# A selective scan beside a mixture of experts: rows added into a DRAM sum, blocks from tile 45 at five tiles each

## The reference

```python
xn = layernorm(x)                                   # x: 2 x 2048 x 256, 4096 tokens in all
delta = softplus(xn @ W_delta.T + delta_bias)       # 256 channels
B_sel, C_sel = xn @ W_B.T, xn @ W_C.T               # 256 channels x 16 states
# for each token in turn, each channel and state:
h = exp(delta*A) * h + (exp(delta*A) - 1)/A * B_t * x_t
y_t = sum over the 16 states of h * C_t
# mixture of 8 experts on the same xn, top 2 per token:
scores = xn @ Wr + br;  w = softmax over the top two
out = sum over the two of w_e * (gelu(xn @ W1[e] + b1[e]) @ W2[e] + b2[e])    # 256 -> 1024 -> 256
result = x + y + out
```

## Time and profile before

| | us |
|---|---|
| median of the runs shown (3 runs) | 1361.06 (1361.04 to 1361.42) |
| the profiled execution's own time | 1359.79 |
| its span, first to last instruction | 1358.1 |
| PE busy | 1196.7 (88%) |
| DVE busy | 917.0 (68%) |
| ACT busy | 819.2 (60%) |
| POOL busy | 758.9 (56%) |
| mean granted TensorE clock | 0.971 |

### The profile page before, as it was taken

One profiled execution on the slowest core, in us unless ns is written; L12 is line 12 of the kernel. 1 busy time (PEld: TensorE's weight loads), 2 busy tenths in 40 slices (PEclk: granted clock), 3 DMA queues, 4 the chain that ended last, 5 costly groups with the idle time before them and its releaser, 6 DMA issues.

```text
span 1358.1 us, 21913 instructions
## 1 busy us (share of the span) xinstructions
PE 1196.7 (88%) x7674; PEld 730.3 (54%) x7674; DVE 917.0 (68%) x1263; ACT 819.2 (60%) x1379; POOL 758.9 (56%) x557
## 2 busy tenths in 40 slices
PE   1567877878899999999999999999999999997664
PEld 0443323333366666666666666666666666663221
DVE  6867878878966566556665565665656655677677
ACT  3655676576487665767666775767666585752110
POOL 2629999999544544354453535435353444446883
PEclk9979999999999999999999999999999999999777
DMA  6693555565324344443334444344444444323651
GB/s 203 200 309 129 180 188 175 190 198 177 118 85 141 125 136 131 152 143 122 125 121 141 140 142 138 125 140 137 125 127 137 152 138 133 106 86 113 190 156 61
DMA packets 95369, 198.03 MB, mean 146 GB/s; under 512 B 13472, under 2 KB 69152, under 8 KB 85280
## 3 DMA queue, kind: packets, MB, share of 16 engines
q1 hardware_dynamic: 89120, 179.91, 41.6%
q0 software_dynamic: 6144, 16.79, 3.7%
HBM read 143.19 MB, written 53.48 MB: 145 GB/s over the span
## 4 chain that ended last, share of the span: by engine, by line
PE 63%; POOL 6%; DVE 3%; issue 2%; DMA 0%; ACT 0%; POOLq 0%; DVEq 0%; SPq 0%
PE bank L1097 31%; PE bank L1161 15%; PE bank L1146 15%; POOL k_xT L946 5%; POOL ax L915 2%; DVE hb L1004 1%; PE bank L1126 1%; PE bank L1172 1%; DVE bank L991 0%; PE bank L1182 0%; DMA ys<-stage 0%; DVE base L1059 0%; DVE base L1043 0%; DVE bank L1016 0%; ACT state L814 0%
## 5 line engine op out<-in xcount | busy, mean ns | idle before, releaser
L915 POOL TENSOR_TENSOR ax<-ax,x 128x512 f32<-128x512 f32 x256 | 325.7, 1274 | 455.6 <-ACT ax L809 452.4
L1097 PE MATMUL bank<-k_xT,k_WB 128*128 128x512 f16 x1536 | 390.1, 392 | 99.1 <-DVE hb L1004 91.4
L991 DVE TENSOR_TENSOR bank<-ax,bank 128x512 f32<-128x512 f32 x256 | 177.8, 695 | 374.6 <-PE bank L1097 238.8
L1097 PE MATMUL bank<-k_xT,k_WC 128*128 128x512 f16 x1536 | 383.5, 387 | 0.7 <-DVE ysum L1026 0.7
L1097 PEld LDWEIGHTS bank<-k_xT,k_WB 128*128 128x128 f16 x1536 | 144.4, 100 | 278.1 <-DVE hb L1004 134.0
L1097 PEld LDWEIGHTS bank<-k_xT,k_WC 128*128 128x128 f16 x1536 | 153.3, 100 | 192.1 <-issue 17.4
L802 ACT ACTIVATE aexp<-k_dcur,k_A 128x512 f32<-128x512 f32 x256 | 180.7, 711 | 109.8 <-DVE hb L1004 106.5
L1004 DVE TENSOR_TENSOR_SCAN hb<-aexp,state,bank 128x512 f32<-128x512 f32 x192 | 244.6, 1274 | 0.0
L1016 DVE SCALAR_TENSOR_TENSOR bank<-hb,k_rA,bank 128x512 f32<-128x512 f32 x240 | 180.0, 750 | 2.4 <-DVE hb L1004 0.9
L1026 DVE TENSOR_TENSOR ysum<-ysum,bank 128x512 f32<-128x512 f32 x240 | 158.8, 662 | 0.0
L809 ACT ACTIVATE ax<-aexp 128x512 f32<-128x512 f32 x256 | 156.9, 614 | 0.0
(11 more groups left out here) (129 smaller groups left out, 1118.0 us busy)
## 6 DMA issues: line engine op xcount, KB each, us to landing
k_x<-wsplit SPq DMA_DIRECT2D x78, 1024.0 KB, 5.1
stage<-in_W SPq DMA_DIRECT2D x32, 512.0 KB, 4.7
wsplit<-stage SPq DMA_DIRECT2D x32, 512.0 KB, 3.2
xs<-k_zero SPq DMA_DIRECT2D x1, 9984.0 KB, 32.0
stage<-xs SPq DMA_DIRECT2D x39, 256.0 KB, 5.0
ys<-stage SPq DMA_DIRECT2D x39, 256.0 KB, 5.7
stage<-in_b SPq DMA_DIRECT2D x39, 128.0 KB, 5.4
k_x<-in_x SPq DMA_DIRECT2D x4, 1024.0 KB, 9.9
```

Source lines behind the costliest of these rows:

```text
L915: nc.gpsimd.tensor_tensor(ax[:, g % MR], ax[:, g % MR], x32[:, hf], ALU.mult).then_inc(ax_done, 1)
L991: v.tensor_tensor(bank, ax[:, g % MR], bank, ALU.mult).then_inc(ux_done, 1)
L1097: ins = mm(bank[:], W[:, a, kc, n, hf * P:(hf + 1) * P], xT[:, c, b, kc, :], start=(k == 1), stop=(k == 3 * KC))
```

## The change

Seven things change together.

- The 64 scatters carry 1040-byte rows: 256 floats' worth of xn and four more, the token's number + 1, its first slot, and the two weights in the form w0 and w1 - w0. `xs` is 260 floats wide, and so is the zeroing DMA. The prologue writes the four columns.
- Five small DVE operations per block (`slot_op`, 128x2 elements) work out from these the weight of each slot and the row of the sum to which it goes (rows beyond the tokens for empty slots). POOL multiplies the block's output by the weights (`add_block`) and adds it into the DRAM tensor `acc` with two accumulating indirect DMAs. `acc` is filled with x by one DRAM-to-DRAM DMA at tile E0 - 3. Each add waits until the ones before it have landed.
- The scan's rows of chunks 0 to 6 are added into `acc` by an accumulating DMA from POOL (`add_rows`), 512 KB each. `ys`, `mid`, the gathers, `add_expert` and the loads and stores around them are gone. At the end `acc` is copied to the output by two DRAM-to-DRAM DMAs, and the last chunk's rows are loaded, completed on DVE and stored.
- E0 = 45, STEP = 5; `down` is cut in three steps of 18, 15 and 15 matmuls; the turn of the next block is at the block's fourth tile. z and the row turns are made by half, and put in a block's first two tiles (`quiet`).
- The 32 pieces of W go at one per 1.25 tiles, with 4 load buffers and 2 store buffers; the odd pieces' low part is made by DVE, the even ones' by POOL. The 64 scatters go at 1.6 per tile (tiles 0 to 39).
- Softplus is made for each half by itself (L829 to L841 before), so there are 14 of them for chunks 1 to 7. The prologue makes `dcur` for both halves.
- `ax` has 4 buffers in place of 5, `ysum` one in place of two, and ACT no longer waits for the zeroing.

```diff
-E0 = 74
-STEP = 4
+E0 = 45
+STEP = 5
+DOWN_AT = (0, 6, 11, 16)
+W_BUF, HL_BUF = 4, 2
...
+def quiet(g):
+    while E0 - 2 <= g < E_END and (g - E0) % STEP > 1:
+        g += 1
+    return g
+Z_AT = {quiet(c * TILES + 13 + 15 * hf): (c + 1, hf) for c in range(NCH - 1) for hf in range(KC)}
+ROW_AT = {quiet(c * TILES + 21 + 16 * hf): (c, hf) for c in range(NCH) for hf in range(KC) if (c, hf) < (NCH - 1, 1)}
...
+def piece_step(k):
+    return k * 5 // 4
+def scatter_step(j):
+    return j * 5 // 8
+def row_add_step(c):
+    return (c + 1) * TILES + (20 if c == 0 else 14)
+def block_add_step(b):
+    return E0 + STEP * b + 13
...
# SP
-        load_piece(0)
-        load_piece(1)
+        for k in range(W_BUF):
+            load_piece(k)
         for g in range(TILE_N):
+            for k in range(SPLITS):
+                if piece_step(k) + 4 == g:
+                    store_piece(k)
+                    if k + W_BUF < SPLITS:
+                        load_piece(k + W_BUF)
+            if g == E0 - 3:
+                sp.dma_start(acc_rows, io["x"].rearrange("b l d -> (b l) d")).then_inc(acc_set, 16)
+                for r in range(HL_BUF):
+                    sp.wait_ge(piece_out[r], SPLITS // HL_BUF * 16)
                 sp.wait_ge(scattered, 2 * NT * 16)
                 load_slots(0)
                 load_slots(1)
                 load_w1(0)
                 load_w2(0)
...
+        sp.wait_ge(added, ADDS * 16)
+        sp.dma_start(base[:], acc_tok[:, LAST_ROWS, :]).then_inc(base_in, 16)
+        # then acc rows 0:2048 and 2048:3584 to the output, then the last rows
...
# POOL
-        pool.wait_ge(keep["zeros_out"], 16)
+        def add_block(b):
+            pool.wait_ge(y_taken, b + 1)
+            pool.wait_ge(w_set, b + 1)
+            nc.gpsimd.tensor_tensor(yo[:, b % 2], yo[:, b % 2], wslot[:, b % 2].unsqueeze(2).broadcast_to([P, BS, D]),
+                                    ALU.mult).then_inc(y_weighted, 1)
+            pool.wait_ge(y_weighted, b + 1)
+            pool.wait_ge(target_set, b + 1)
+            pool.wait_ge(added, ADD["block", b] * 16)
+            for s in range(BS):
+                nc.gpsimd.indirect_dma_start(
+                    out=io["acc"], out_offset=bass.IndirectOffsetOnAxis(target[:, b % 2, s:s + 1], 0),
+                    in_=yo[:, b % 2, s], in_offset=None, compute_op=ALU.add).then_inc(added, 16)
+        def add_rows(c):
+            pool.wait_ge(turn_taken, USE["row", c, KC - 1] + 1)
+            ...
+            nc.gpsimd.dma_start(acc_tok[:, chunk_tokens(c), :], base[:], accum_op=ALU.add).then_inc(added, 16)
         for g in range(TILE_N):
             times_x(g)
+            if g == 0:
+                pool.wait_ge(keep["zeros_out"], 16)
...
# DVE
+        def low_piece(k):
+            dve.wait_ge(p_hi, k + 1)
+            v.tensor_tensor(whl[:, k % HL_BUF, 1, :], wst[:, k % W_BUF, :], whl[:, k % HL_BUF, 0, :],
+                            ALU.subtract).then_inc(p_lo[1], 1)
...
             if g + 1 < TILE_N:
                 ux_op(g + 1)
+            for k in range(STEP):
+                if block_at(g, k) is not None:
+                    slot_op(block_at(g, k), k)
             scan_op(g)
             if g >= 1:
                 acc_op(g - 1)
+            for k in range(1, SPLITS, 2):
+                if piece_step(k) + 3 == g:
+                    low_piece(k)
             hc_op(g)
```

More of the change, by code:

```diff
@@ L541, in turn_bank_uses @@
     for g in range(TILE_N):
+        if g in ROW_AT:
+            order.append(("row",) + ROW_AT[g])
+        if g in Z_AT:
+            order.append(("z",) + Z_AT[g])
         if turn_block(g) is not None:
             order.append(("turn", turn_block(g)))
[L544 to L548, removed]
     return {name: i for i, name in enumerate(order)}
@@ L561, in tile_banks, with adds_before @@
     return bank, before
+def piece_step(k):
[6 more added lines that the diff above has]
+    return E0 + STEP * b + 13
+def adds_before():
+    count, n = {}, 0
+    for g in range(TILE_N):
+        for c in range(NCH - 1):
+            if row_add_step(c) == g:
+                count["row", c] = n
+                n += 1
+        for b in range(NBLK):
+            if block_add_step(b) == g:
+                count["block", b] = n
+                n += BS
+    return count, n
 def expert_of(eng, keep, b):
@@ L866, in high_h @@
             nc.scalar.activation(hs[b % 2][:, 0, fs, :], h32[:, fs, :], ACT.Copy).then_inc(hi_done, 1)
-        act.wait_ge(keep["zeros_out"], 16)
         for g in range(LEAD):
             exp_tile(g)
-        for g in range(LEAD - 1):
+        for g in range(MR - 1):
             less_one(g)
         for g in range(TILE_N):
-            c, s = divmod(g, TILES)
-            first, second = block_at(g, 1), block_at(g, 2)
+            first, late = block_at(g, 1), block_at(g, 2)
             if first is not None:
@@ L878, in _ @@
                 high_h(first, 0)
-            if second is not None:
-                gelus(second, 1)
-                high_h(second, 1)
+            if late is not None:
+                gelus(late, 1)
+                high_h(late, 1)
                 if g - 1 + LEAD < TILE_N:
@@ L1030, in take_y @@
             if b >= 2:
-                dve.wait_ge(y_out[b % 2], b // 2 * 16)
+                dve.wait_ge(added, (ADD["block", b - 2] + BS) * 16)
             v.scalar_tensor_tensor(yo[:, b % 2], Yps[:].rearrange("p (s d) -> p s d", d=D), 1.0 / WSCALE,
@@ new lines, in take_rows, with last_rows @@
+        def take_rows(c, hf):
+            dve.wait_ge(turn_made, USE["row", c, hf] + 1)
+            if hf == 0 and c >= 1:
+                dve.wait_ge(added, (ADD["row", c - 1] + 1) * 16)
+            v.tensor_scalar(base[:, :, hf * P:(hf + 1) * P], Tps[:].rearrange("p (q d) -> p q d", q=CT),
+                            1.0 / (WSCALE * WSCALE), None, ALU.mult).then_inc(turn_taken, 1)
+        def last_rows(hf, bank):
+            dst = base[:, :, hf * P:(hf + 1) * P]
+            v.scalar_tensor_tensor(dst, bank[:].rearrange("p (q d) -> p q d", q=CT), 1.0 / (WSCALE * WSCALE), dst,
+                                   ALU.mult, ALU.add).then_inc(turn_taken, 1)
@@ L1073, in _ @@
                 acc_op(g - 1)
+            for k in range(1, SPLITS, 2):
+                if piece_step(k) + 3 == g:
+                    low_piece(k)
             hc_op(g)
[L1075 to L1078 removed]
         acc_op(TILE_N - 1)
[L1080 to L1085 removed]
+        dve.wait_ge(base_in, 16)
+        dve.wait_ge(turn_made, USE["row", NCH - 1, 0] + 1)
+        last_rows(0, Tps)
+        dve.wait_ge(y_made, NBLK + 1)
+        last_rows(1, Yps)
     @block.tensor
```

467 lines of the change are left out of this document (208 added, 259 removed).

## The result

The change makes the kernel slower: 1372.77 us (median of 4 runs, 1371.64 to 1374.87) against 1361.22 (1361.04 to 1361.42) on the same chip; the ratio is 1.0087 with a 95% interval of [1.0069, 1.0104]. I had said 1330 and a range of 1304 to 1352. The execution that was profiled took 1372.12 on a span of 1370.4.

The account below looks back on a forecast made before the run. POOL was taken to bound the front, PE the expert blocks. 316.5 to the first hidden matmul + 963 + 6 + 42.2 at the end = 1327.7 us of span, 1330 as measured time; range 1304 to 1352.

Parts of the forecast that it names:

- The middle: First hidden matmul to PE's last down: 963 us, plus 6 for slot_op and row adds together.
- rival 3: Expert tiles: slot_op between ux and scan holds the scan; decides from 0.19 us net per tile; 12% together with 4.
- a slack of 0.8 to 1.8: Expert blocks: us by which waits of slot_op, between ux and scan, could be hidden.
- PE's arithmetic: Expert stage: 39 blocks at 23.87 us give 930.9; with the remaining tiles, z projections and row turns, 963 used.
- The start: Prologue: three small copies cost 0.65 us, the zeroing nothing; first times_x moves from 101.28 to 101.9.
- Stage A: Tiles 0 to 41: POOL is the bound, losing 9 us to DVE's odd pieces; scan 41 at 283.5.
- The seam: Tiles 43 to 45: the copy of x takes 20 us and holds block 0's loads; first hidden matmul at 316.5.
- The end: From PE's last down to the end, without gathers: 42.2 us.
- 1: Rival at tiles 43 to 45: cheap, copy shorter or not holding the loads, no POOL loss; 1306 to 1323; 20%.
- 2: Rival in the front: full lock +10, copy at 26 +6, late zeros +7, up to 1353; 18%.
- 4: Rival in the blocks: a DRAM add takes over 24 us, each block waits, 1400 or more; 12% together with rival 3.

Follow-up runs that it names:

- E5: The kernel after with slot_op on DVE at the same place, as one-column operations with one tensor input in SBUF: 1334.70 us, 0.9804 of before.
- G3: The kernel before with one small two-SBUF-input DVE operation added between ux and scan in each of 156 expert tiles: 1362.16 us, 1.0003.
- F3: E5 with the copy of x into the sum issued behind block 0's loads: 1322.38 us, 0.9721 of before.
- G4: F3 with the block's add issued ahead of the chunk's row add at POOL: 1322.65 us, 0.9717 of before.
- E4: The kernel after with the odd W pieces' low part back on POOL: 1386.47 us, 1.0188 of before.

## Why the prediction was wrong

**The middle: the step that failed.** "From nothing to 58 us (0.3 net on 195); I take 6 for them and the row adds together." It was 37 (38 by the difference to E5, 0.19 us net on each of 195, which is rival 3's own threshold). The rival's place, mechanism and threshold were right; I gave it and another 12% together. Two things led me astray. I argued with an average wait of 0.4 us against a slack of 0.8 to 1.8; the average is about right (134.8 / 195 - 0.15 = 0.54), but the waits last to the end of a POOL operation: about half of the operations wait for nothing, and L1078, which meets `low_h` in the block's fourth tile, waits 1.3 on average. What PE loses is the part above the slack, and this is set by the long ones: above the 0.8 of the prediction itself it adds up to the 42 of the estimate under G3. And I took DVE's 1.5 us of waiting for PE per tile as slack; it is the slack of steps of 5.2 us. G3 shows that there it would have sufficed.

**The row that was misread.** The earlier trace rows has a pair of DVE operations at 6.02 us "where one alone took 2.23". The one was not alone. POOL's operation beside it is missing from the rows:

```profile
39.13 4.21 POOL L262 TENSOR_TENSOR k_x<-xcur,k_x 128x1024 f32 x2 [2.58 <-ACT k_x L308]
42.19 2.23 DVE L382 SCALAR_TENSOR_TENSOR k_WB<-stB,k_WB 128x1024 f32 x1 [1.44 <-ACT k_WB L298]
44.33 2.13 POOL L270 TENSOR_TENSOR k_WC<-stC,k_WC 128x1024 f32 x1 [0.99 <-ACT k_WC L302]
45.25 2.29 DVE L382 SCALAR_TENSOR_TENSOR k_WB<-stB,k_WB 128x1024 f32 x1 [0.83 <-ACT k_WB L298]
```

Both operations end 1.08 us after POOL's (43.34 and 46.46): each waited for POOL to end and then took its own 1.1. The pair of 6.02 is two such, 3.0 each. So the trace of before shows a full wait for the POOL operation under way, a wait that has nothing to do with the DVE operation's own length. For the pieces of W the prediction took it for a mutual slowing of some 0.6 a piece; for `slot_op` it named the wait of up to 2.14 and then argued it away with the mean.

**PE's arithmetic** (963 for 39 blocks and what lies between) was right: PE is busy 964.1 of E5's 968.2.

**The start.** The first `times_x` came at 103.42, not 101.9. Not the three copies' own time, but the wait of one of them: L451 lasted 2.33 us beside POOL's add to `dcur` (2.34), which the prediction named as lying under them. Then the zeroing, costed at nothing because it had been over in time and had the same bytes: 3.5 us.

**Stage A.** Scan 41 at 295.34, not 283.5. POOL's order and its being the bound were right; its list was short. Scatters 73.0 + 13.6 instead of 75.3 (+11.3), waits for ACT (+7.8), zeroing (+3.1), against 9 that I had set aside for the lock. The lock's 9.9 us in the scatters were not in my count of victims: I had looked only at arithmetic. That it comes so near to the 9 is luck, since the arithmetic lost only 1.2.

**The seam.** The copy took 15.6 us, not 20, and held the loads as said. That it was shorter hid a part of stage A's 11.8 us: the first hidden matmul is late by only 7.6, which is luck and not a better front. The order of the two DMAs cost 9 to 12 us of PE (F3). The prediction had priced this (302 against 308.6 for the slots) and the mechanism held. From the turn to the first hidden matmul it took 8.2 us and not 6.6, as PE came back at the lower clock.

**The end** was right: 40.4 us for 42.2.

**The other rivals.** 1 fell: the copy did hold the loads. 2 came true in part (zeros, lock in the front) and gave 7.6 of its 23. 4 fell as a bound: with E5's `slot_op` the adds' waits are hidden (G4). In the kernel after they were not quite: the two longest waits of `slot_op` stand right behind two of them.

**The best version** is H1: E5's `slot_op`, the late copy, five `ax` buffers, the zeroing at multiples: 1315.95, 0.9669 of before. The change's idea is worth 45 us; as built, 195 two-column operations (38 us), the order of the copy (12), the zeroing (4) and the missing `ax` buffer (2) spent 57.

## What to carry to other kernels

A tiny DVE operation with two inputs in SBUF can cost what POOL is doing at that moment, not what it computes; before you put one between a producer and the operation that a busy PE waits for, give it another form (here one column and one tensor input) or another engine, and look in the trace whether that form waits too. Measure slack at the shortest step of the new schedule, and add up what the single waits exceed it by; their mean tells nothing. Before you call a row "alone", look at what the other engines do in its time. A row that grows by a few bytes changes where each later run begins: price that on every large DMA that walks over such rows.

## What the runs showed of the hardware

- A DVE operation with two inputs in SBUF waited until POOL's operation under way had ended (1.08 us of its own after it, in the prologue of before; 2.11 beside 2.12 for two columns). It need not come next: two of 195 small ones let a run of POOL operations without a gap go first (5.05 and 7.52 us), and five of 16 long ones did (3.49 to 5.73). POOL's pace did not change.
- POOL's issue of an indirect DMA took 1.79 to 1.86 us where a two-input DVE operation was running, some 0.99 otherwise.
- One input is no safeguard by itself: a copy of 128x32 took 2.33 us beside POOL, 0.20 in E4, where POOL had ended.
- `tensor_scalar` with one tensor in SBUF and its other operands as scalars by pointer took 205 to 266 ns a column on average at the same places, never over 271, against means of 154 to 1411 for the two-column form with two.
- A DRAM-to-DRAM copy of 4.19 MB took 15.6 and 16.6 us, 18.5 beside other loads; 260 KB loads issued behind it landed after 14.1 instead of 5.3.
- The same zeroing of 10.4 MB took 44.5 to 46.5 us in runs of 1040 or 2028 bytes that begin off multiples of 1024, and some 32 in runs of 1024 on them.
